# Slot lookups of a GNN kernel moved into GpSimd's pause between two convolutions

## The reference

```python
for l in range(thetas.shape[0]):
    xi = x[src]
    xj = x[dst]
    e = jax.nn.relu((xj - xi) @ thetas[l].T + xi @ phis[l].T)
    agg = jax.ops.segment_max(e, src, num_segments=N)
    agg = jnp.where(agg < -1e+30, 0.0, agg)
    mu = agg.mean(axis=0)
    var = agg.var(axis=0)
    x = jax.nn.relu((agg - mu) * jax.lax.rsqrt(var + BN_EPS) * gammas[l] + betas[l])
```

## Time and profile before

| | |
|---|---|
| Time, median of 3 runs | 1787.68 us (1783.46 to 1789.74) |
| The profiled execution's own time | 1791.4 us |
| Its span | 1789.6 us |
| Busy: PE, DVE, ACT, POOL | 1078.7, 1239.0, 986.2, 956.0 us |
| Mean granted clock of PE | 0.834 of full speed |
| Convolution 0, gathers on POOL | 704.0 to 948.8 us of the span |
| Convolution 1, POOL's first instruction to the next pause | 981.6 to 1193.7 us |
| Convolution 2, POOL's first gather | 1236.2 us |

### The profile page before, as it was taken

How to read it: one execution, slowest core, us unless ns; L and a number is a source line. 1 busy time by engine, 2 the same in 40 slices (tenths; PEclk the granted TensorE clock), 3 DMA queues, 4 the chain that set the end, 5 groups by cost and what they waited for, 6 DMA issues and landing times.

```text
span 1789.6 us, 16599 instructions
## 1 busy us (share of the span) xinstructions
PE 1078.7 (60%) x3823; PEld 561.4 (31%) x3823; DVE 1239.0 (69%) x2657; ACT 986.2 (55%) x2630; POOL 956.0 (53%) x1013
## 2 busy tenths in 40 slices
PE   0148987870006561899998599897999988000000
PEld 0023333320003331455554355454445444000000
DVE  8848776778978992355454256453666678889998
ACT  4736876664555774344434355554455544666665
POOL 1057766667767777777772777622554227640000
PEclk9999998995557875899999799998999999555555
DMA  8277899997694673688885377865966459999999
GB/s 368 101 228 231 288 326 358 325 302 245 191 324 131 215 232 121 195 264 257 259 263 178 81 166 186 170 169 126 137 142 133 105 153 278 420 416 383 397 402 390
DMA packets 174965, 431.98 MB, mean 241 GB/s; under 512 B 28308, under 2 KB 107682, under 8 KB 154900
## 3 DMA queue, kind: packets, MB, share of 16 engines
q1 hardware_dynamic: 107748, 227.24, 36.3%
q0 software_dynamic: 43904, 98.91, 22.2%
q10 hardware_dynamic: 23216, 104.77, 16.9%
HBM read 254.11 MB, written 180.72 MB: 243 GB/s over the span
## 4 chain that ended last, share of the span: by engine, by line
PE 32%; DVE 23%; DMA 20%; POOL 11%; issue 8%; ACT 4%; SPq 2%; ACTq 0%; POOLq 0%; DVEq 0%
PE ps L1288 11%; PE ps L1301 11%; DMA out<-arena 7%; POOL arena L1240 5%; DMA arena<-x 5%; PE ps L1278 3%; POOL arena L858 3%; DVE arena L1557 2%; PE ps L1465 2%; DVE stat L804 2%; DMA arena<-last_of 2%; DVE arena L1542 2%; DMA x_dst<-arena 2%; DMA arena<-x,idx 2%; ACT arena L843 2%
## 5 line engine op out<-in xcount | busy, mean ns | idle before, releaser
L1373 DVE TENSOR_TENSOR_SCAN arena<-arena,ps 128x512 f32<-128x512 f32 (+1 forms) x150 | 187.0, 1254 | 266.6 <-PE ps L1288 228.5
L858 POOL DMA_INDIRECT arena<-x,idx x196 | 186.0, 949 | 183.0 <-DVE idx L622 90.9
L1259 POOL DMA_INDIRECT arena<-agg,slot x196 | 185.3, 946 | 174.2 <-PE ps L1278 79.8
L1301 PE MATMUL ps<-arena 128*128 128x512 f32 x600 | 270.7, 595 | 10.5 <-ACT arena L1343 10.5
L1288 PE MATMUL ps<-arena 128*128 128x512 f32 x600 | 271.3, 596 | 7.1 <-DVE arena L1373 7.1
L1240 POOL DMA_INDIRECT arena<-x,idx x196 | 185.4, 946 | 61.0 <-issue 58.2
L1570 ACT ACTIVATE ps<-arena 128x256 f32<-128x256 f32 x391 | 143.7, 368 | 94.2 <-DVE arena L1542 94.2
L843 ACT ACTIVATE arena<-arena,shift,inv 128x256 f32<-128x256 f32 (+1 forms) x311 | 156.1, 586 | 50.7 <-DVE shift L835 34.0
L1377 DVE TENSOR_TENSOR ps<-arena,ps 128x512 f32<-128x512 f32 (+1 forms) x150 | 101.7, 683 | 97.0 <-PE ps L1301 96.7
L1343 ACT ACTIVATE arena<-big,bn_shift,bn_scale 128x512 f32<-128x512 f32 (+1 forms) x100 | 75.1, 798 | 164.1 <-PE ps L1301 152.5
L1301 PEld LDWEIGHTS ps<-arena 128*128 128x128 f32 x600 | 115.9, 194 | 151.9 <-issue 140.3
(11 more groups left out here) (214 smaller groups left out, 2126.7 us busy)
## 6 DMA issues: line engine op xcount, KB each, us to landing
arena<-x SPq DMA_DIRECT2D x39, 1280.0 KB, 9.6
out<-arena SPq DMA_DIRECT2D x39, 1280.0 KB, 11.7
arena<-x ACTq DMA_DIRECT2D x31, 1280.0 KB, 10.4
x<-arena ACTq DMA_DIRECT2D x31, 1280.0 KB, 6.2
agg<-arena SPq DMA_DIRECT2D x48, 512.0 KB, 4.0
arena<-not_same SPq DMA_DIRECT2D x72, 256.0 KB
arena<-last_of SPq DMA_DIRECT2D x72, 256.0 KB
x_dst<-arena SPq DMA_DIRECT2D x24, 512.0 KB, 3.8
```

Source lines behind the costliest of these rows:

```text
L858: pl.indirect_dma_start(rows_in[:, par, a, g, :], None, x[:, :], bass.IndirectOffsetOnAxis(ap=idx[:, k, t * G + g:t * G + g + 1], axis=0)) ...
L1259: pl.indirect_dma_start(conv_in[:, b, 1, g, :], None, agg_dram[l - 1][:, :], bass.IndirectOffsetOnAxis(ap=slot[:, t * G + g:t * G + g + 1] ...
L1301: m = pe.matmul(near_bank[j][:, 0:width(t)], thp[:, l, 1, k, j * P:(j + 1) * P], near_t[:, par, k, 0:width(t)], start=(k == 0), stop=(k == 1))
L1373: v.tensor_tensor_scan(runmax[:, par, j, 0:width(t)], mask[:, tl % 2, 0:width(t)], far_bank[j][:, 0:width(t)], initial, ALU.add, ALU.max). ...
```

## The change

Of the 54 lookups that stood inside convolution 1, 20 (`SLOTS_PAUSE` = 5 tiles of four columns) are now issued at the head of `later_pool(1)`, ahead of the wait for `s_agg_ready`, and count to `s_slot_got`. The other 34 are issued two per tile, in tiles 2 to 18. The wait for late lookups stands now at tiles 16 and 21, for 20 and 14 lookups, where it stood at tiles 11 and 18 for 28 and 26. The number of lookups, their data and every other engine's instructions stay as they were.

```diff
         SLOTS_EARLY = 11
-        SLOTS_STEPS = 7
+        SLOTS_PAUSE = 5
+        SLOTS_STEPS = 5
+        SLOTS_FIRST = SLOTS_EARLY + SLOTS_PAUSE
...
         def later_pool(pl, l):
+            if l == 1:
+                for c in range(SLOTS_EARLY * G, SLOTS_FIRST * G):
+                    slot_lookup(pl, c, s_slot_got)
             pl.wait_ge(s_agg_ready, l)
             if l == 1:
                 pl.wait_ge(s_x1s_ready, 1)
-                pl.wait_ge(s_slot_got, 16 * G * SLOTS_EARLY)
+                pl.wait_ge(s_slot_got, 16 * G * SLOTS_FIRST)
...
                     for k in range(2):
-                        if t == SLOTS_EARLY + k * SLOTS_STEPS:
-                            pl.wait_ge(s_slot_late[k], 16 * min(G * SLOTS_STEPS, NC - G * (SLOTS_EARLY + k * SLOTS_STEPS)))
-                    for c in range(3 * t + min(t, 2), min(3 * t + min(t, 1) + 4, NC - G * SLOTS_EARLY)):
-                        slot_lookup(pl, SLOTS_EARLY * G + c, s_slot_late[c // (G * SLOTS_STEPS)])
+                        if t == SLOTS_FIRST + k * SLOTS_STEPS:
+                            pl.wait_ge(s_slot_late[k], 16 * min(G * SLOTS_STEPS, NC - G * (SLOTS_FIRST + k * SLOTS_STEPS)))
+                    if t >= 2:
+                        for c in range(2 * (t - 2), min(2 * (t - 1), NC - G * SLOTS_FIRST)):
+                            slot_lookup(pl, SLOTS_FIRST * G + c, s_slot_late[c // (G * SLOTS_STEPS)])
                 pl.wait_ge(s_conv_turned, turns_before(l, max(t - RC + 1, 0)))
```

## The result

The changed kernel takes 1768.38 us (median of four runs, 1765.81 to 1770.15), the kernel before in the same set 1788.71 (1783.46 to 1801.36): a ratio of 0.9875, 95% interval 0.9846 to 0.9903, so 20.3 us faster. A later set, with six and 25 runs, gave 1766.66 against 1788.36, ratio 0.989, interval 0.9865 to 0.9915. The profiled execution took 1768.92 us with a span of 1767.1.

The account below looks back on a forecast made before the run. POOL was taken to bound convolution 1's first five tiles, PE the later ones. 14.7 us up to tile 5 plus 8.8 for the mask stall gave 23.5, from 1791.4 to 1767.9 or 1764.2; forecast 1766, range 1759 to 1779.

Parts of the forecast that it names:

- The lookups in the pause: GpSimd's pause before convolution 1: 20 lookups take 25.0 of 32.85 us, leave 7.5 and cost 0.
- the rival of lookups that don't fit: Pause before convolution 1: lookups outlast it, from 1.64 us each; at 3.0 each the time is 1794; chance 2%.
- The five-fold price: Lookups in the pause: descriptor generation locked out by DVE's 2-port mode, 20 lookups taking 95 us, turning the sum into a loss.
- Tiles 0 to 2: Head of convolution 1: fewer lookups ahead of the gathers, PE turns tile 2 at 1002.0, not 1013.06; gain 11.1 us.
- Tiles 3 to 5: Convolution 1, after the head: PE's 2.74 us wait at tile 4 and 1.4 us of slower period go, less 0.5.
- late tile 3: Convolution 1, tile 3: with a landing of 6.86 us its gather would be 1.3 us late; 0.5 subtracted.
- The mask stall: Convolution 1, after the last lookup: 16 back-to-back gathers make a mask late; without the burst 8.8 us go, 0 at the other end.
- the ring: Convolution 1: POOL gains 1.12 us a tile and meets the full ring near tile 17 or 18, leaving no room for a burst.
- The moved bulk waits: Waits for late lookups at tiles 16 and 21, four tiles after the last lookup they cover: cost nothing.
- The shares of the queues: DMA engines before tile 18: POOL's queue at 42%, with SP's 37.4% some 79%, against 93% in the stall.
- the first rival: Convolution 1: the mask stall stays or moves, only the head's 14.7 us are gained; 1775 us; chance 28%.
- the other end of that choice: Whole time: the profiled execution's 3.7 us above the median belong to the stalls that go, so the median ends near 1767.9.

Follow-up runs that it names:

- s_after: The changed kernel, nothing altered, run again in a later set for a second usable profile: 1766.66 us, ratio 0.989 to the kernel before.
- e1: Changed kernel, but the 34 late lookups come three per tile (tiles 2 to 13), not two: 1776.41 us, ratio 0.9946 to the kernel before.
- s_e5: Changed kernel, but of the 34 late lookups four stand in tile 0, four in tile 1, then two per tile to tile 14: 1776.46 us, ratio 0.9935.
- e2: Changed kernel, but no lookups in the pause; all 54 come three per tile in tiles 2 to 19: 1773.67 us, ratio 0.9944 to the kernel before.
- e4: Kernel before plus 23 spare lookups in tiles 17 to 24, into a tile that nothing reads: 1781.38 us, ratio 0.9978.
- e6: Kernel before with three mask buffers, not two, each mask load issued a tile earlier: 1782.42 us, ratio 0.9976.
- s_before: The kernel before, nothing altered, run again in the later set for a second usable profile: 1790.03 us, ratio 1.0009.
- e3: Changed kernel, but all 54 lookups stand ahead of the wait, none inside the convolution: 1800.3 us, ratio 1.0079 to the kernel before.

## Why the prediction was right, step by step

**The lookups in the pause** cost nothing, as forecast: 25 us under 32.85, with 7.76 left (forecast 7.5). They took 0.94 to 0.95 us each beside DVE's work at the end of convolution 0, so the rival of lookups that don't fit is out. The five-fold price that I took from the Trainium skill ("SBUF — State Buffer", section "SBUF: two separate sides") is for DVE in a 2-port mode; no row here shows which mode DVE was in, so these rows bear out that the price did not arise, and not that the rule is wrong. The pause ended at 982.03 and not 981.62, but its length is the better measure. From POOL's last gather of convolution 0 to its first instruction after the wait it took 32.4 to 32.9 us in the four profiles with lookups in it (after, s_after, e1, s_e5) and 31.7 to 32.9 in the five without, so the lookups did not lengthen it by more than it varies.

**Tiles 0 to 2.** Forecast 11.1 us, measured 10.8 and 11.1 (31.44 to 20.66, 31.10 to 19.95). e2 and e5 show the cause.

**Tiles 3 to 5.** Forecast 2.7 + 1.4 - 0.5 = 3.6, measured 4.6 and 3.1. PE turned tile 5 at 1028.54, forecast 1028.5. The prediction had both causes in its sum, the earlier head and the step of 7.5 us, but did not part them, and my expectation for e1 counted on the head alone. e1 has that head and still waits 2.77 us at tile 4, because at three lookups a tile POOL is at 8.75 us a tile and gains nothing on PE. Its last gather for tile 4 is issued 3.9 us before PE is due and takes 6.8 to land; in the changed kernel it is issued 6.66 us before PE's turn, in s_after 6.00, and PE does not wait. The 0.5 us that I took off for a late tile 3 did not arise.

**The mask stall.** Forecast 8.8, measured 8.8 and 11.0 (of the latter 9.7 at tiles 20 and 21, the rest small waits for gathers at tiles 10 to 17). The mechanism was argued from rows alone and held: the stall moves with the last lookup (e1, e2), goes with spare lookups (e4), and goes with earlier masks though the burst stays (e6). POOL first waits for the ring at tile 17 (0.72 us at 1107.39), as forecast. The moved bulk waits have no part in it: in s_before the one at tile 18 held POOL for 2.57 us, in the first profile not at all, and PE waited for no gather behind it.

**The shares of the queues** were mis-sized. I scaled 35.8% by the rate to 42%, and with SP's to 79%; measured were 50.6% and 88.3%. A gather cost more DMA time when gathers came more densely. That is close to the 93% of the stall, and still no mask was more than 4.2 us late. So the share did not tell a stall from none; the margin against the first rival was smaller than I had written, and its 28% were not too many. The argument against that rival, that gathers of convolution 2 run at four per 5 us, held only for its head: in the kernel before POOL waits some 3 us a tile for the ring from 1273.43 on, so they come four per 7.74 us, and the longest late mask there (5.87 us, at 1287.91) falls into that part, at nearly the 7.5 us of the changed kernel. What parts the cases is how long DVE stood for a mask: up to 4.2 us here and 6.2 in e3 cost PE nothing, 8.0 in e1 and 8.6 in s_before did. The prediction had no such limit, so that the masks stayed within it is in part luck.

**The sum.** Forecast 23.5 for the stage, measured 24.1 and 25.5. The spans fell by 22.5 (1789.6 to 1767.1) and 28.2 (1786.3 to 1758.1): 24.1 less 0.4 by which the stage began later and 1.2 that the rest took longer, and 25.5 plus 5.3 less 2.6. The medians of the runs fell by 20.3 and 21.7. The forecast of 1766 took half of the 3.7 us by which the profiled execution stood above the median as not being part of the stalls; 1768.38 is what the other end of that choice gives (1767.9). Why the medians fell by some 4 us less than the stage stays open: only the profiled executions show their stages, and what lies ahead of the stage varies by some 11 us among them, what follows it by 8 (550.3 to 558.6).

## What to carry to other kernels

An engine that issues at almost exactly the rate of the engine that it feeds builds up no lead, and every slow landing becomes a wait; take out of each round what makes its pace clearly faster (7.5 against 8.62 us here, not 8.75), and use a pause for what that pushes out. Look at what stands ahead of the first items of a stage before anything else: eight lookups there cost 10 us, and the same eight in tiles 15 to 18, where the changed kernel has them and e5 has none, nothing. Where an interleaved side job ends, look for the burst of the main one and for the short-notice loads that it delays; one more buffer for those loads cured that (some 9 us of the stage, 6 of the time) without touching the burst.

## What the runs showed of the hardware

The DMA time of a gather was not constant. For each MB that POOL's queue moved, its packets took 6.0 us of all 16 engines in the kernel before (35.8% of 86 us for 5.14 MB), 7.3 in the changed kernel (50.6% of 87 us for 6.04 MB), lookups included in both, 8.3 in e3 (79.5% of 26 us for 2.49 MB) and 8.8 in the burst of the kernel before (64.6% of 20 us for 1.47 MB); a gather is 0.13 MB. So the denser the gathers came, the more each cost. The Trainium skill ("DMA: Bandwidth & Descriptors", section "Issuing engines are not separate DMA queues") says that the DMAs of all issuing engines run interleaved on the same 16 engines. The stores on SP's queue agree: they took 3.8 and 4.5 us to land while lookups and gathers alternated, before and after the change, and 14.7 in the burst of the kernel before. That last figure varies: in the bursts of s_before and e6 it was 6.8 and 6.9.
